# Gated delta rule on one core: VectorE's level 5 copies between the halves of q's convolution, TensorE's level 5 products ahead of the turned outputs

## Chip, cores and metric

The kernel runs on one core of a Trainium2 chip. The metric is the device time of one execution in microseconds (us); lower is better. The chip's engines are TensorE (PE in the rows; PEld is its weight load), VectorE (DVE), ScalarE (ACT), GpSimd (POOL) and SyncE (SP). Each takes its instructions in program order, and they wait for each other by semaphores.

## What is computed

The program is a stack of eight blocks on x (8 batches of 256 tokens, 128 features), each of the form x = x + layernorm(block(layernorm(x))). The change touches only the first, the gated delta rule attention. Cut to what matters:

```python
q, k = l2norm(silu(conv4(h @ w_q))), l2norm(silu(conv4(h @ w_k)))   # 16 heads of 64
v = silu(conv4(h @ w_v))                                            # 16 heads of 128
def step(S, inp):                       # one token
    q_t, k_t, v_t, g_t, b_t = inp
    S = S * exp(g_t)
    delta = (v_t - k_t @ S) * b_t
    S = S + outer(k_t, delta)
    return S, (q_t * scale) @ S
y = rmsnorm(o) * norm_w * silu(h @ w_g)
out = y @ w_out
```

conv4 is a causal convolution over four tokens, each feature with its own four taps.

## The kernel before

The function `gated_delta` (line 1869) works in chunks of 128 tokens (two in a batch, index `c`) with four heads at a time (`hg`). One unit of work is a quad: a batch and a group of four heads, 8 x 4 = 32 in all. `quads` (line 1922) writes the same pipeline into every engine: `step(x0, x1, x2, x3)` handles four quads at once, x0 being the newest and x3 the oldest. There are 35 steps; in 29 of them both x0 and x3 exist, and in the last three x0 is gone. Steps of the batches from the second on stand in a loop of four steps.

What sets the order of the work is the text of the five `step` functions, written out by hand: an engine does the calls in exactly that order. The parts that the change and the prediction touch are these.

- `project(x0, n)` on TensorE (line 1983): the projections of quad x0 into PSUM, n = 0 for q, 1 for k, 2 and 3 for v. Bank 4 holds n = 0 and 2, bank 5 holds n = 1 and 3. `project(x0, 2)` waits until ScalarE has copied both turned outputs out of bank 4 (semaphore `yT`).
- `tap3` on ScalarE (L2282) writes the fourth tap's share of the convolution into SBUF, two tiles of 128x256 (index `m`). `conv(x0, n)` on VectorE (L2544) adds the other three taps: for each tap two `scalar_tensor_tensor`, one for each m, and between taps a `drain`, because the next tap reads what the last one wrote. It then raises `conv`.
- The inverse of a 128x128 triangular matrix is put together from blocks of 16, of 32 and of 64; the code counts these as levels 4, 5 and 6. Of level 5: `merge_y(x2, 1, c)` on TensorE (L2083) multiplies into banks 0 and 1; `step_5(x2, c)` on VectorE (L2581, L2582) copies these to SBUF; `merge_t(x2, 1, c)` on TensorE (L2105) multiplies the copies into banks 2 and 3; `copy_t(x2, 1, c)` on ScalarE (L2334, L2335) brings them to SBUF; `turn_64` on VectorE (L2587) transposes a block. `merge_y(x2, 2, c)` (L2086) needs that for level 6.
- `turn_y(x0, x3, 1)` on TensorE (L2176): four transposes of x3's finished outputs into bank 4. It waits for `conv(x0, 0)`, which reads bank 4. `copy_y(x3, 1)` on ScalarE (L2381) takes them out. `out` on TensorE (L2189) multiplies them with `w_out` into bank 5; it waits for `copy_y(x3, 1)` and for `conv(x0, 1)`, which reads bank 5.
- `silu_qk` (L2295, with a table load of its own) and `square_qk` (L2302) on ScalarE follow the convolutions of q and k; between the two stands `tap3(x0, 2)`. `sum_squares` on TensorE (L2018) needs the squares.
- On SyncE and GpSimd the blocks of 16 are inverted; the order there is not touched.

ScalarE's order at this place is `tap3(x0, 1)`, `copy_y(x3, 1)`, `copy_t(x2, 1, 0)`, `copy_t(x2, 1, 1)`, `silu_qk(x0)`, `tap3(x0, 2)`, `square_qk(x0)`.

Of the kernel before, what the change touches and what calls it, by code (L numbers as in the profile page):

```python
# [1868 lines left out]
def gated_delta(k, add_y):  # L1869
# [13 lines left out]
    with Part(k) as p:  # L1883
# [29 lines left out]
        q = {n: p.sem(n) for n in names}  # L1913
# [3 lines left out]
        def wait(eng, name, n):  # L1917
            if isinstance(n, int) and n <= 0:
                return
            eng.wait_ge(q[name], n)  # L1920
# [14 lines left out]
        def first(x):  # L1935
            return isinstance(x[1], int) and x[1] == 0
# [7 lines left out]
        def halves_of(a, s):  # L1944

            a = a.rearrange("p (n two s) -> p n two s", two=2, s=s)
            return a[:, :, 0, :], a[:, :, 1, :]
# [4 lines left out]
        with nc.Block() as block:  # L1952
# [25 lines left out]
            def _(pe):  # L1978
# [110 lines left out]
                def merge_t(e, l, c):  # L2089
                    qe, b, hg = e  # L2090
                    s = (16, 32, 64)[l]
                    wait(pe, "Ystep", 6 * qe + 2 * l + c + 1)
                    if l == 2:
                        wait(pe, "TTc", 4 * qe + c + 1)
                    pe.sem_inc(q["through_pe"], 1)
                    for h in range(HG):
                        cols = slice(h * 64, (h + 1) * 64)
                        t = TT[:, hg % 2, c, h, :]
                        if l == 0:
                            i = mm(k.bank[2 + c][:, cols].rearrange("p (n s) -> p n s", s=s), step4[:, c, h, :], halves_of(t, s)[1],  # L2100
                                   start=True, stop=True)
                        elif l == 1:
                            for n in range(2):
                                r = slice(64 * n, 64 * n + 64)
                                i = mm(k.bank[2 + c][r, h * 64 + 32 * n:h * 64 + 32 * n + 32], step5[r, c, h, r],  # L2105
                                       t[r, 64 * n + 32:64 * n + 64], start=True, stop=True)
                        else:
                            i = mm(k.bank[2 + c][0:64, cols], step6[64:, c, h, 0:64], t[64:, 64:], start=True, stop=True)
                    i.then_inc(q["TTps"], 1)
# [54 lines left out]
                def turn_y(a, e, c):  # L2164
                    qe = e[0]
                    wait(pe, "y", 2 * qe + c + 1)
                    if c == 0:
                        wait(pe, "gate", 2 * qe + 1)
                        if a is not None:
                            wait(pe, "vtok", 2 * a[0] + 1)  # L2170
                    elif a is not None:
                        wait(pe, "conv", 4 * a[0] + 1)
                    else:
                        wait(pe, "yT", 2 * qe + 1)
                    for h in range(HG):
                        i = tr(hd(4, h), v[:, e[2], c, h, :], k.ident[:])  # L2176
                    i.then_inc(q["yTps"], 1)
# [23 lines left out]
                def step(x0, x1, x2, x3):  # L2201
                    if x0:
                        decays(x0, 0)
                    if x3:
                        turn_y(x1, x3, 0)
                    if x1:
                        turn_v(x1, 1)
                    if x2:
                        merge_y(x2, 0, 0)
                        merge_y(x2, 0, 1)  # L2210
                        merge_t(x2, 0, 0)
                        merge_t(x2, 0, 1)
                    if x0:
                        project(x0, 0)
                        decays(x0, 1)
                    if x3 and x3[2] == 0 and not first(x3):
                        turn_out(x1, x3[1] - 1)
                    if x2:
                        merge_y(x2, 1, 0)
                        merge_y(x2, 1, 1)  # L2220
                    if x0:
                        project(x0, 1)
                    if x3:
                        turn_y(x0, x3, 1)
                    if x2:
                        merge_t(x2, 1, 0)
                        merge_t(x2, 1, 1)
                    if x0:
                        project(x0, 2)
                    if x3:  # L2230
                        out(x0, x1, x3)
                    if x2:
                        merge_y(x2, 2, 0)
                        merge_y(x2, 2, 1)
                        merge_t(x2, 2, 0)
                    if x0:
                        sum_squares(x0)
                    if x2:
                        solve(x2, 0)
                        project_gate(x0, x2, 0)  # L2240
                    if x0:
                        turn_norms(x0)
                        turn_k(x0)
                        project(x0, 3)
                    if x2:
                        merge_t(x2, 2, 1)
                    if x0:
                        products(x0, 0)
                    if x2:
                        state(x2)  # L2250
                        outputs(x2, 0)
                        from_state(x2)
                    if x0:
                        products(x0, 1)
                    if x2:
                        solve(x2, 1)
                        project_gate(x0, x2, 1)
                    if x0:
                        turn_v(x0, 0)
                    if x2:  # L2260
                        outputs(x2, 1)
# [253 lines left out]
            def _(dve):  # L2515
# [17 lines left out]
                    dve.sem_inc(q["through_dve"], 1)  # L2533
                    vv.tensor_copy(xb[:], k.HT[:, bass.ds(b, 1), PAD:].rearrange("p a t -> p (a t)")).then_inc(q["xb"], 1)

                def conv(a, n):
                    qa, b, hg = a
                    wait(dve, "tap3", 4 * qa + n + 1)
                    first = (hg * 2, 8 + hg * 2, 16 + hg * 4, 18 + hg * 4)[n]
                    for j in (2, 1, 0):  # L2540
                        back = 3 - j
                        for m in range(2):
                            dst = (qk[:, hg, m], qk[:, hg, 2 + m], vT[:, m], vT[:, 2 + m])[n]
                            i = stt(out=dst[:, back:], in0=k.bank[4 + n % 2][:, m * T:(m + 1) * T - back],  # L2544
                                    scalar=taps[:, first + m, j:j + 1], in1=dst[:, back:], op0=ALU.mult, op1=ALU.add)
                        if j:
                            dve.drain()
                    i.then_inc(q["conv"], 1)

                def turn_blocks(e, name):  # L2550
                    hg = e[2]
# [38 lines left out]
                def step_6(e, c):  # L2590
                    wait(dve, "Yps", 6 * e[0] + 4 + c + 1)
                    vv.tensor_copy(step6[64:128, c, :, 0:64], packed(c, 64)[64:128, :, 0, :]).then_inc(q["Ystep"], 1)
# [77 lines left out]
                def step(x0, x1, x2, x3):  # L2670
                    if x0 and x0[2] == LAG:
                        load_x(x0)
                    if x2:
                        step_4(x2, 0)
                    if x3:
                        sum_o(x3, 1)
                    if x2:
                        step_4(x2, 1)
                        add_4(x2, 0)
                        add_4(x2, 1)  # L2680
                        dve.drain()
                        turn_blocks(x2, "T32")
                    if x3 and x3[2] == 0 and not first(x3):
                        copy_out(x3[1] - 1)
                    if x0:
                        conv(x0, 0)
                    if x2:
                        step_5(x2, 0)
                        step_5(x2, 1)
                    if x0:  # L2690
                        conv(x0, 1)
                    if x2:
                        turn_64(x2)
                        step_6(x2, 0)
                    if x0:
                        conv(x0, 2)
                    if x3:
                        add_y(x3)
                    if x2:
                        step_6(x2, 1)  # L2700
                    if x0:
                        norms(x0)
                        conv(x0, 3)
                        mask_products(x0, 0)
                    if x2:
                        subtract_memory(x2)
                        sum_o(x2, 0)
                    if x0:
                        mask_products(x0, 1)
                    if x1:  # L2710
                        turn_16(x1)
                    if x2:
                        add_o(x2)
# [768 lines left out]
```

## Time and profile before

| | us |
|---|---|
| three runs | 4843.22, 4853.23, 4852.27; median 4852.27 |
| the profiled execution: its own time | 4854.47 |
| its span in the profile | 4852.3 |
| steps with x0 and x3, start of `out` to the next start of `out` | 36.3 where nothing disturbs |
| VectorE busy in 400 to 600 us | 155.0 of 200 |
| TensorE busy in 400 to 600 us | 173.2 of 200 |

The gated delta rule lies between about 46 and 1310 us of the span. All rows come from one profiled execution. A row of the timeline gives start, duration, engine, line, operation, output and inputs, and the number of instructions that are merged in it; in brackets stands the idle time of the engine just before it and what ended that.

### The profile page before, as it was taken

To read this page: it belongs to the slowest core of one execution; us is meant where nothing else is said; L and a number is where in the kernel's file an instruction comes from. 1 tells how busy PE (TensorE), PEld (TensorE's weight loads), DVE (VectorE), ACT (ScalarE), POOL (GpSimd) and SP (SyncE) were. 2 spreads that over 40 slices of the span, in tenths; PEclk is the share of its full clock that TensorE was granted. 3 is DMA by queue.
4 is the path that set the end of the run, shared out by engine and by line. 5 is a ranking of instruction groups with operands and counts; after the bars stand their busy time and mean duration, and the time that the engine had idled before them with its cause. 6 is when DMAs were issued, how large, how long until landed. Compare 5 with 4: busy or idle time off the path is not lost. (4 is left out here: it accounts for less than half of the span.)

```text
span 4852.3 us, 76307 instructions
## 1 busy us (share of the span) xinstructions
PE 3918.1 (81%) x20245; PEld 2363.5 (49%) x20365; DVE 3743.4 (77%) x6391; ACT 2514.1 (52%) x5271; POOL 2862.3 (59%) x2779
## 2 busy tenths in 40 slices
PE   5888888888568678577989965888888868888885
PEld 3666666666456456466447742333333323333333
DVE  5777777777468478456058867999999889999996
ACT  3555555555344244323246644666666556666662
POOL 2555555555454044143023342999999559999992
PEclk7999999999778778788999986999999989999997
DMA  1000000000000000000000000000000000000000
GB/s 50 9 9 9 8 9 9 9 9 9 17 0 0 21 0 0 12 0 25 0 18 1 1 16 16 0 0 0 0 0 0 0 0 0 0 0 0 0 0 14
DMA packets 89949, 33.35 MB, mean 7 GB/s; under 512 B 78016, under 2 KB 85968, under 8 KB 88784
## 3 DMA queue, kind: packets, MB, share of 16 engines
q1 hardware_dynamic: 89680, 30.07, 2.6%
q8 instruction: 131, 2.15, 0.2%
q14 instruction: 138, 1.13, 0.1%
HBM read 24.79 MB, written 5.24 MB: 6 GB/s over the span
## 5 line engine op out<-in xcount | busy, mean ns | idle before, releaser
L3319 POOL TENSOR_TENSOR dBx<-dtx,b_row 128x1024 f32<-128x1024 f32 x512 | 1207.1, 2358 | 3.9 <-ACT b_row L3285 3.9
L3353 DVE TENSOR_TENSOR_SCAN h<-banks,dBx 128x1024 f32<-128x1024 f32 x512 | 1168.4, 2282 | 19.1 <-ACT banks L3279 19.1
L3237 PE MATMUL banks<-hc,ident 128*128 128x512 f32 x2048 | 965.5, 594 | 0.0
L3279 ACT ACTIVATE banks<-dt,alog 128x510 f32<-128x510 f32 x1024 | 661.6, 682 | 3.6 <-DVE h L3353 3.6
L3285 ACT ACTIVATE b_row<-banks 128x512 f32<-128x512 f32 x512 | 305.7, 597 | 575.8 <-PE banks L3221 575.8
L3237 PEld LDWEIGHTS banks<-hc,ident 128*128 128x128 f32 x2048 | 389.1, 190 | 271.9 <-issue 246.9
L3361 DVE TENSOR_TENSOR hc<-h,banks 128x768 f32<-128x768 f32 x512 | 478.4, 934 | 11.0 <-ACT c_row L3290 7.5
L3221 PE MATMUL banks<-bc_lo,selectors 128*128 128x512 bf16 x1024 | 391.9, 383 | 67.6 <-POOL b_row L3308 58.7
L3328 POOL TENSOR_TENSOR hc<-h,c_row 128x256 f32<-128x256 f32 x512 | 373.2, 729 | 63.2 <-ACT c_row L3290 29.3
L3220 PE MATMUL banks<-bc_hm_c,selectors 128*128 128x512 bf16 x506 | 195.2, 386 | 184.4 <-DVE hc L3361 184.3
L3220 PEld LDWEIGHTS banks<-bc_hm_c,selectors 128*128 (+1 forms) x512 | 49.2, 96 | 433.7 <-issue 433.6
L973 POOL TENSOR_TENSOR weighted<-probs,f 128x1024 f32<-128x1024 f32 x64 | 120.7, 1902 | 215.1 <-DVE f L1024 211.3
L2488 POOL TENSOR_TENSOR out_factors<-out_norms,exponents 128x4 f32<-128x4 f32 x64 | 64.4, 1007 | 289.1 <-DVE out_norms L2653 289.1
L3221 PEld LDWEIGHTS banks<-bc_lo,selectors 128*128 (+1 forms) x1024 | 99.7, 97 | 185.1 <-issue 168.4
L2544 DVE SCALAR_TENSOR_TENSOR qk<-banks,taps,qk 128x255 f32<-128x255 f32 (+2 forms) x384 | 167.2, 477 | 26.9 <-ACT qk L2282 15.4
L2544 DVE SCALAR_TENSOR_TENSOR v_featmajor<-banks,taps,v_featmajor 128x255 f32<-128x255 f32 (+2 forms) x384 | 167.3, 477 | 22.0 <-ACT v_featmajor L2282 11.4
L1642 POOL TENSOR_TENSOR squares<-qkv_ahead 128x1024 f32<-128x1024 f32 x32 | 60.9, 1904 | 183.9 <-ACT qkv_ahead L1578 183.9
L159 POOL MEMSET minus_half<- 128x4 f32 x7 | 0.7, 102 | 279.5 <-POOLq L365 162.9
L3220 PE MATMUL banks<-bc_hm_b,selectors 128*128 128x512 bf16 x398 | 153.0, 385 | 4.1 <-ACT b_row L3285 4.1
L2464 POOL TENSOR_TENSOR blocks_inv<-blocks_inv,block_products 64x14 f32<-64x14 f32 (+6 forms) x448 | 117.2, 262 | 63.7 <-issue 0.3
L2462 POOL TENSOR_TENSOR block_products<-blocks_inv,blocks 64x14 f32<-64x14 f32 (+6 forms) x448 | 114.0, 254 | 67.0 <-issue 5.5
L1211 POOL TENSOR_TENSOR norms<-norms,minus_half 128x64 f32<-128x64 f32 x8 | 84.7, 10593 | 105.9 <-DVE norms L1242 105.9
(448 smaller groups left out, 9091.8 us busy)
## 6 DMA issues: line engine op xcount, KB each, us to landing
delta_blocks<-A_turned SPq DMA_DIRECT2D x256, 8.0 KB, 1.5
inv_turned<-delta_blocks SPq DMA_DIRECT2D x256, 8.0 KB, 1.7
blocks<-delta_blocks SPq DMA_DIRECT2D x32, 64.0 KB, 2.1
delta_blocks<-blocks_inv SPq DMA_DIRECT2D x32, 64.0 KB, 1.9
wh<-in_l1f_wh SPq DMA_DIRECT2D x1, 2048.0 KB, 9.3
wqkv<-in_l0f_wqkv SPq DMA_DIRECT2D x2, 768.0 KB, 4.3
residual<-in_x SPq DMA_DIRECT2D x1, 1024.0 KB, 4.7
wv<-in_l0a_wv SPq DMA_DIRECT2D x1, 1024.0 KB, 7.5
```

The source lines that it names most:

```text
L973: nc.gpsimd.tensor_tensor(blocks(SW[:, u]), blocks(S[:, j % 2, u]), over(f[:, j % 2, 16 * u:16 * u + 16], T // NJ), ALU.mult).then_inc(wei ...
L2464: i = tt(U[:, 0:j, j + 1:], U[:, 0:j, j + 1:], tmp[:, 0:j, 0:n], ALU.add)
L2544: i = stt(out=dst[:, back:], in0=k.bank[4 + n % 2][:, m * T:(m + 1) * T - back], scalar=taps[:, first + m, j:j + 1], in1=dst[:, back:], op ...
L3220: nc.tensor.matmul(k.bank[bank], onto_all(sel[:, 0, bass.ds(n, 1)]), mem[part][:, cols], start=True, stop=False)
L3221: nc.tensor.matmul(k.bank[bank], onto_all(sel[:, which, bass.ds(n, 1)]), mem["lo"][:, cols], start=False, stop=True).then_inc(q[ready], 1)
L3237: i = nc.tensor.matmul(k.bank[e], k.ident[:], hc[:, s, e, :], start=False, stop=False)
L3279: i = nc.scalar.activation(a3[:, :, 1:], d3[:, :, 1:], ACT.Exp, scale=mem["A"][:, e, bass.ds(n, 1)])
L3285: nc.scalar.activation(bsb[:, s, :], k.bank[BBANK], ACT.Copy).then_inc(q["bsb_ready"], 1)
L3319: nc.gpsimd.tensor_tensor(dBx[:, s % NS], dtx[:, :, bass.ds(c * SCH, SCH)], across(bsb[:, s % NS, :], SE), ALU.mult).then_inc(q["dbx_ready ...
L3328: nc.gpsimd.tensor_tensor(hc[:, s % 2, :, DC:], h[:, s % NS, :, DC:], across(csb[:, s % 2, :], SE), ALU.mult).then_inc(q["hcp_ready"], 1)
L3353: v.tensor_tensor_scan(flat(h[:, s % NS]), flat(k.banks[:, at:at + SE, :]), flat(dBx[:, s]), 0.0, ALU.mult, ALU.add).then_inc(q["scanned"], 1)
L3361: v.tensor_tensor(hc[:, s % 2, :, 0:DC], h[:, s, :, 0:DC], across(k.bank[CBANK][:, 0:DC], SE), ALU.mult).then_inc(q["hc_ready"], 1)
```

## The change

On VectorE the two halves of `conv(x0, 0)` (m = 0 and m = 1) are done one after the other, and the four copies of `step_5` stand between them. A half is three `scalar_tensor_tensor` with a drain after the first and the second. The semaphore `conv` is raised after the second half. On TensorE `merge_t(x2, 1, 0)` and `merge_t(x2, 1, 1)` come before `turn_y(x0, x3, 1)` and not behind it. The other engines are as before.

```diff
@@ TensorE, step
                     if x0:
                         project(x0, 1)
-                    if x3:
-                        turn_y(x0, x3, 1)
                     if x2:
                         merge_t(x2, 1, 0)
                         merge_t(x2, 1, 1)
+                    if x3:
+                        turn_y(x0, x3, 1)
                     if x0:
                         project(x0, 2)
@@ VectorE
-                def conv(a, n):
+                def conv(a, n, parts=(0, 1)):
                     qa, b, hg = a
                     wait(dve, "tap3", 4 * qa + n + 1)
...
                     for j in (2, 1, 0):
                         back = 3 - j
-                        for m in range(2):
+                        for m in parts:
...
                         if j:
                             dve.drain()
-                    i.then_inc(q["conv"], 1)
+                    if 1 in parts:
+                        i.then_inc(q["conv"], 1)
@@ VectorE, step
                     if x0:
-                        conv(x0, 0)
+                        conv(x0, 0, (0,))
                     if x2:
                         step_5(x2, 0)
                         step_5(x2, 1)
                     if x0:
+                        conv(x0, 0, (1,))
                         conv(x0, 1)
```

## Rows read from the trace of the kernel before

**Rows 1.** The page's part 1: busy us, share of the span, instructions.

```profile
PE 3918.1 (81%) x20245; PEld 2363.5 (49%) x20365; DVE 3743.4 (77%) x6391; ACT 2514.1 (52%) x5271; POOL 2862.3 (59%) x2779
```

**Rows 2.** Waits from 100 to 1240 us: us in total, times, longest.

```profile
PE banks L2189 <- DVE qk L2544: 27.9, 29, 1.1
```

**Rows 3.** Timeline of TensorE, one step.

```profile
709.86 1.12 PE L2083 MATMUL banks<-inv,A_turned 64*64 64x32 f32 x32 [0.49 <-DVE inv L2554]
710.91 1.13 PE L2002 MATMUL banks<-norm_featmajor,wk 128*128 x4
712.57 0.66 PE L2176 MATMUL banks<-ident,v 128*128 128x128 f32 x4 [0.52 <-DVE qk L2544]
713.28 1.28 PE L2105 MATMUL banks<-inv_turned,steps 64*64 64x32 f32 x32
714.49 1.13 PE L2002 MATMUL banks<-norm_featmajor,wv 128*128 x4
716.61 1.99 PE L2189 MATMUL banks<-y_featmajor,wout 128*128 128x256 f32 x8 [0.99 <-DVE qk L2544]
718.53 1.14 PE L2086 MATMUL banks<-inv,A_turned 64*64 64x64 f32 x16
```

**Rows 4.** Timeline of VectorE, the same step.

```profile
707.41 0.42 DVE L2576 TENSOR_TENSOR inv_turned<-banks,inv_turned 128x256 f32<-128x256 f32 x1 [0.92 <-PE banks L2100]
707.93 1.79 DVE L2554 STREAM_TRANSPOSE inv<-inv_turned 32x256 f32<-32x256 f32 x4
709.75 2.76 DVE L2544 SCALAR_TENSOR_TENSOR qk<-banks,taps,qk 128x255 f32<-128x255 f32 x6
712.54 0.28 DVE L2581 COPY steps<-banks 32x128 f32<-32x128 f32 x1
...
713.46 0.30 DVE L2582 COPY steps<-banks 32x128 f32<-32x128 f32 x1
713.79 2.76 DVE L2544 SCALAR_TENSOR_TENSOR qk<-banks,taps,qk 128x255 f32<-128x255 f32 x6
716.58 0.43 DVE L2587 STREAM_TRANSPOSE inv<-inv_turned 32x256 f32<-32x256 f32 x1
```

**Rows 5.** Timeline of VectorE: the first three instructions of q's convolution, one by one.

```profile
709.75 0.48 DVE L2544 SCALAR_TENSOR_TENSOR qk<-banks,taps,qk 128x255 f32<-128x255 f32 x1
...
710.15 0.47 DVE L2544 SCALAR_TENSOR_TENSOR qk<-banks,taps,qk 128x255 f32<-128x255 f32 x1
...
710.70 0.48 DVE L2544 SCALAR_TENSOR_TENSOR qk<-banks,taps,qk 128x254 f32<-128x254 f32 x1
```

**Rows 6.** Timeline of ScalarE, the same step.

```profile
713.26 0.60 ACT L2381 ACTIVATE y_featmajor<-banks 128x512 f32<-128x512 f32 x1 [0.25 <-PE banks L2176]
713.97 0.27 ACT L2334 ACTIVATE inv_turned<-banks 32x128 f32<-32x128 f32 x1
...
715.16 1.28 ACT L2295 ACT_TABLE_LOAD   x1
716.59 1.06 ACT L2295 ACTIVATE qk<-qk 128x1024 f32<-128x1024 f32 x1
...
718.40 1.05 ACT L2302 ACTIVATE squares<-qk 128x1024 f32<-128x1024 f32 x1
```

**Rows 7.** Timeline of TensorE: the sum of squares in that step.

```profile
720.39 0.81 PE L2018 MATMUL banks<-squares,halves 128*8 128x256 f32 x3
```

**Rows 8.** Stretches around 599 us: length, engines busy, granted clock, DMA.

```profile
595.77:599.18 3.41, 2.28 (x38) 1.85 (x38) 3.14 (x10) 2.14 (x6) 2.16 (x9) 1.00 0.01 2
599.20:602.60 3.40, 3.10 (x8) 1.99 (x7) 2.12 (x5) 3.20 (x6) 2.30 (x8) 0.50 0.02 5
```

**Rows 9.** Timeline of TensorE at that place.

```profile
596.97 0.66 PE L2176 MATMUL banks<-ident,v 128*128 128x128 f32 x4 [1.07 <-DVE qk L2544]
...
598.89 1.82 PE L2002 MATMUL banks<-norm_featmajor,wv 128*128 x4
601.01 2.76 PE L2189 MATMUL banks<-y_featmajor,wout 128*128 128x256 f32 x8 [0.30 <-DVE qk L2544]
...
605.57 1.68 PE L2018 MATMUL banks<-squares,halves 128*8 128x256 f32 x7
```

**Rows 10.** Timeline of TensorE in the last steps, without x0.

```profile
1237.20 1.11 PE L2176 MATMUL banks<-ident,v 128*128 128x128 f32 x4
1238.24 1.92 PE L2105 MATMUL banks<-inv_turned,steps 64*64 64x32 f32 x32
1240.09 3.78 PE L2189 MATMUL banks<-y_featmajor,wout 128*128 128x256 f32 x8
```

## The prediction

> **What bounds the kernel now.** The page's busy shares come first [rows 1]: TensorE 81%, VectorE 77%. Neither is full, so the two must be handing a chain to each other, and the question is who waits for whom at the edited place. The waits answer it: `out` (L2189) waited for a convolution on VectorE 29 times, 27.9 us in all, nearly a microsecond each [rows 2]. The 29 are all the steps that have both x0 and x3.
>
> The timelines of one step show the place. On VectorE one stretch without a gap runs from 707.41, where TensorE released it, to 717.01: the last addition of level 4, its transposes, q's convolution at 709.75, the four copies of level 5 from 712.54 to 713.76, k's convolution from 713.79 to 716.55, and the transpose of 32 [rows 4]. On TensorE there are two idle gaps beside it: 0.52 us before `turn_y`, which waits for q's convolution, and 0.99 us before `out`, which waits for k's [rows 3]. After `out` TensorE goes on almost without a gap. So between 707.4 and 716.6 VectorE sets the time, and from 716.6 TensorE does. The gap ahead of `turn_y` lies inside the stretch where TensorE has a further 0.99 us to spare; it costs nothing today.
>
> **What is moved.** The copies start earlier by half a convolution, and the products (1.28 us [rows 3]) can run in the old gap. But `out` still waits for k's convolution, and that ends when VectorE has done the same instructions as before. I take the parts in turn.
>
> *The split of q's convolution, on the path.* Six instructions come in three pairs. Within a pair the second starts 0.40 us after the first (709.75, 710.15), though each takes 0.48; over a drain the next starts 0.55 us after (710.15 to 710.70) [rows 5]. Before, the way from the first start to the first copy is 0.40, 0.55, 0.40, 0.55, 0.40 and, from the last start to the copy, 0.50: 2.80 in all (the rows give 2.79, 709.75 to 712.54 [rows 4]). After, each half has two gaps of 0.55, since each instruction now has the drain behind it. First half: 0.55 + 0.55 + 0.50 = 1.60, copies at 711.35. The copies hold the engine 1.25 us (712.54 to 713.79 [rows 4]): second half at 712.60. Its third instruction starts at 713.70, and k's convolution, which does not depend on it, 0.40 later: 714.10 and not 713.79. So VectorE ends k's convolution 0.30 us later. That is 32 quads x 0.30 = 9.6 us, all on the path. From below, the drains could be hidden, 0; from above, a single instruction could pay its full 0.48 plus the 0.15 that the drain adds to 0.40, hence 0.63 a gap: 4 x 0.08 x 32 = 10 us more. I take 0.30, since 0.55 is measured on the same instruction with the same drain.
>
> [...]
>
> *Waits queued on VectorE.* The second half of q's convolution now stands behind `step_5`'s wait for `merge_y`. That ends at 710.98 [rows 3], and the copies are reached at 711.35, so nothing. Its own repeated wait is long satisfied.
>
> *TensorE up to `out`, covered.* The first product can start at about 712.0 (copies of c = 0 done at 711.9), the second after 712.6; they end near 713.25. Then `turn_y` waits: q's convolution now ends at 713.70 + 0.47 = 714.17, where it was 712.51, so `turn_y` starts at 714.22. `copy_y` started 0.69 us after `turn_y` (712.57, 713.26 [rows 3, 6]): 714.91 to 715.51. `project(x0, 2)` must wait for it, as both use bank 4: 715.57 to 716.70. `out` wants k's convolution, 716.85, and starts at 716.91. So the later transposes are hidden by 0.2 us; if that cover were gone, each further 0.1 us would cost 2.9 us in all.
>
> *ScalarE, nearly on the path.* `copy_t` stands behind `copy_y`: it moves to 715.5, the four copies take 1.1 us, and then the table load (1.28), which was over just in time at 716.44, ends at 717.8. `silu_qk` starts there, 0.95 us later than k's convolution would let it. From the start of `silu_qk` to the end of the squares is 2.86 us (716.59 to 719.45 [rows 6]), so squares are ready at 720.66. `sum_squares` would be reached by TensorE at 720.39 + 0.30 = 720.69 [rows 7]. A tie: 0, at most 0.1 x 29 = 3 us. `turn_64` needs `copy_t` by 716.9 and gets it at 716.5: nothing.
>
> *The last steps.* Without x0 the products (1.92) and the transposes (1.11 [rows 10]) change places, and `out` must wait for a copy of 0.6 us behind the transposes: about 0.7 us in each of two steps, 1.4.
>
> *The clock.* Before `out` TensorE's granted clock sometimes falls to 1.2 GHz. In the stretch ending at 599.18 TensorE was busy 2.28 us of 3.41, with a gap of 1.07 before `turn_y`, and in the next the granted clock is 0.50 [rows 8, 9]. It happened in 2 of the 29 steps. The price: `out` to `sum_squares` took 4.56 us (601.01 to 605.57) against 3.78 (716.61 to 720.39) [rows 7, 9], so 0.78 each, and `project(x0, 2)` took 1.82 and not 1.13 us [rows 3, 9]. After the change the gaps in this place are 0.97 and 0.68 and 0.2 us, with only the small products and four transposes between the two projections, which stand 3.5 us apart (2.45 before: 712.04 to 714.49). That is thinner work than in any of the steps before, so I expect the fall in about half of the 29 steps, at 0.8 us or a little more as the slow projection now eats its 0.2 us cover: 14 x 0.9 = 13 us. Falls elsewhere in the step (at the start of level 4) shift with the step's length; I take 2 us back for these. Net 11, between -5 and +25.
>
> The sum: 9.6 + 1.4 + 0 + 11 = 22 us. The profiled execution took 4854.5, which is 2.2 above the median shown; on the median of 4852.3 this gives **4874 us**.
>
> **The rivals.**
> 1. *The split alone costs, and the clock stays as it is.* 4852.3 + 11 = 4863. For it: the longest single gap is 0.97 us and these exist today. Against: there are now two of them. 18%.
> 2. *Clock and ScalarE together.* The clock falls in nearly every step and the squares are late: 29 x 1.0 + 3 + 11 = 43, 4895. 8%.
> 3. *Faster: the filled gap counts.* If the 0.52 us ahead of `turn_y` were on the path, 29 x 0.52 = 15 us would come back, less the split: 4848, or 4837 with a free split. It decides from the point where k's convolution is ready before TensorE reaches `out`, so that TensorE and not VectorE sets its start. Rows 2 and 3 show the opposite in all 29 steps. A shift of the clock's falls could do the same. 6%. The Trainium skill says ("Perfetto Trace Analysis", Optimizing Scalar/DVE Operations) that breaking up instructions can help where VectorE is not saturated but leaves bubbles on others; over the whole span it isn't, in these 9.6 us it is.
> 4. *It does nothing: drains are free and everything else is covered.* 4852 to 4856. [...] 10%.
> The forecast has the remaining 58%, with its own range 4866 to 4883.
>
> **The numbers.** A measurement of this kernel can tell about 0.2% (9.7 us) from no change, so "same" is 4842.6 to 4862.0. Faster: rival 3, 6%. Same: rival 4 and something under half of rival 1, 17%. Slower: the rest, 77%. The range from 4857 to 4888 leaves out rivals 2 and 3 and part of 4.
>
> **What would show it.** In the changed profile: single instructions of q's convolution 0.55 us apart; k's convolution starting 4.35 us after q's (4.04 before [rows 4]); the wait of `turn_y` (L2176) for L2544 near 1 us and not 0.5; a new wait of L2002 for `copy_y`; `silu_qk` right behind its table load; steps of 36.6 us where nothing disturbs, 36.3 before; and more stretches at clock 0.50 just before `out`. If `out` no longer waits for L2544, or undisturbed steps keep their length, the forecast's reasons are wrong.

## The result and the profile after

The changed kernel takes 4915.78 us (median of four runs, 4909.88 to 4921.96), the kernel before 4852.75 (four runs, 4843.22 to 4856.25). The ratio is 1.0133 with a 95% interval of 1.0113 to 1.0153: 63 us slower, where 22 us were forecast. The direction was right; the time lies outside the range. Of all executions behind this document one, of the kernel e2 below, was in a slower state (8530.74 us); it counts in no median and no ratio.

The page after (busy us; the span in 40 slices, PEclk is the granted TensorE clock in tenths), to set against [rows 1]:

```profile
PE 3971.1 (81%) x20245; PEld 2401.0 (49%) x20365; DVE 3747.6 (76%) x6391; ACT 2511.4 (51%) x5271; POOL 2862.8 (58%) x2779
PEclk7999988999868788779899987899999989999997
```

VectorE has the same 6391 instructions and 4 us more work. TensorE has the same number of instructions too, yet is busy 53 us longer. Work that stays equal and takes longer points to the clock. Here is the same stretch, 124 to 1200 us, in both kernels (the third last number is the granted clock as a share of 2.4 GHz). Before:

```profile
124.00:1200.00 1076.00, 937.03 (x7416) 689.06 (x7416) 820.45 (x2283) 609.25 (x1379) 616.21 (x1222) 0.97 0.06 9
```

After:

```profile
124.00:1200.00 1076.00, 933.84 (x6967) 687.80 (x6965) 772.15 (x2139) 571.22 (x1295) 579.96 (x1160) 0.91 0.05 8
```

In the same time TensorE did 449 fewer matmuls (6%) while it was equally busy; VectorE did 144 fewer instructions.

**A step in which the clock stays up** is as forecast, but for one gap on VectorE. TensorE after, around 510 us, to set against [rows 3]:

```profile
506.42 1.13 PE L2002 MATMUL banks<-norm_featmajor,wk 128*128 x4
507.60 1.28 PE L2105 MATMUL banks<-inv_turned,steps 64*64 64x32 f32 x32
510.12 0.66 PE L2176 MATMUL banks<-ident,v 128*128 128x128 f32 x4 [1.24 <-DVE qk L2544]
511.56 1.10 PE L2002 MATMUL banks<-norm_featmajor,wv 128*128 x4 [0.78 <-ACT y_featmajor L2381]
512.80 1.99 PE L2189 MATMUL banks<-y_featmajor,wout 128*128 128x256 f32 x8
...
516.68 1.89 PE L2018 MATMUL banks<-squares,halves 128*8 128x256 f32 x8
```

The products now run at once, and the gap has moved: 1.24 us before `turn_y` and a new 0.78 us before `project(x0, 2)`, which waits for the copy. VectorE in that step, to set against [rows 4]:

```profile
505.25 1.59 DVE L2544 SCALAR_TENSOR_TENSOR qk<-banks,taps,qk 128x255 f32<-128x255 f32 x3
506.86 0.28 DVE L2582 COPY steps<-banks 32x128 f32<-32x128 f32 x1
...
508.11 1.04 DVE L2544 SCALAR_TENSOR_TENSOR qk<-banks,taps,qk 128x255 f32<-128x255 f32 x2
509.59 3.16 DVE L2544 SCALAR_TENSOR_TENSOR qk<-banks,taps,qk 128x253 f32<-128x253 f32 x7 [0.44 <-issue]
512.78 0.43 DVE L2588 STREAM_TRANSPOSE inv<-inv_turned 32x256 f32<-32x256 f32 x1
```

The second and third instruction of the first half, looked at one by one as in [rows 5]; the first starts at 505.25:

```profile
505.81 0.48 DVE L2544 SCALAR_TENSOR_TENSOR qk<-banks,taps,qk 128x254 f32<-128x254 f32 x1
...
506.37 0.48 DVE L2544 SCALAR_TENSOR_TENSOR qk<-banks,taps,qk 128x253 f32<-128x253 f32 x1
```

These starts are 0.56 us apart. The step has one thing more: the row at 509.59 shows VectorE idle for 0.44 us in the middle of the second half, and what ended that is "issue", so it waited for nothing that the profile shows. It is no accident of this step. Between the last addition of level 4 and `out`, on the stretch where VectorE sets the time, the kernel before has no such gap in any of its 29 steps. The changed one has 18, in 18 steps, of 0.43 to 0.49 us: 14 inside q's convolution and 4 ahead of a copy that comes just before it. A start over a drain then comes 0.92 us after the last one and not 0.56, so such a gap costs 0.36 us. Here is one ahead of the copy, from e3 below, and then the same copy before:

```profile
916.51 0.42 DVE L2679 COPY block_out<-banks 128x256 f32 x1 [0.48 <-issue]
746.08 0.42 DVE L2668 COPY block_out<-banks 128x256 f32 x1
```

ScalarE in that step, to set against [rows 6]:

```profile
510.82 0.60 ACT L2381 ACTIVATE y_featmajor<-banks 128x512 f32<-128x512 f32 x1 [2.31 <-PE banks L2176]
...
512.43 1.28 ACT L2295 ACT_TABLE_LOAD   x1
513.72 1.06 ACT L2295 ACTIVATE qk<-qk 128x1024 f32<-128x1024 f32 x1
...
515.53 1.05 ACT L2302 ACTIVATE squares<-qk 128x1024 f32<-128x1024 f32 x1
```

`silu_qk` starts right behind its table load and 0.92 us after `out`; the squares end at 516.58, and `sum_squares` starts at 516.68, 3.88 us after `out`. Before, this was 3.76 to 3.88. So ScalarE costs next to nothing.

**A step in which the clock falls** looks like this. TensorE, one step later, to set against [rows 7, 9]:

```profile
546.78 0.66 PE L2176 MATMUL banks<-ident,v 128*128 128x128 f32 x4 [0.88 <-DVE qk L2544]
548.21 2.04 PE L2002 MATMUL banks<-norm_featmajor,wv 128*128 x4 [0.78 <-ACT y_featmajor L2381]
550.05 3.62 PE L2189 MATMUL banks<-y_featmajor,wout 128*128 128x256 f32 x8
...
555.89 1.89 PE L2018 MATMUL banks<-squares,halves 128*8 128x256 f32 x8
```

Its stretches, as in [rows 8]:

```profile
544.12:547.50 3.38, 2.39 (x39) 1.61 (x37) 3.14 (x9) 1.02 (x4) 2.12 (x9) 1.00 0.01 2
547.53:550.90 3.37, 2.69 (x6) 2.18 (x7) 2.18 (x5) 3.29 (x7) 2.23 (x9) 0.50 0.02 5
550.95:554.30 3.35, 3.35 (x14) 2.34 (x12) 0.00 (x0) 2.27 (x4) 2.07 (x9) 0.50 0.01 2
554.36:557.70 3.34, 3.10 (x28) 1.75 (x26) 2.88 (x7) 0.38 (x1) 2.05 (x3) 1.00 0.11 22
```

The granted clock is 0.50, that is 1.2 GHz, from 547.5 to 554.3. The projection takes 2.04 us and not 1.10, and only behind it `out` can start, 1.84 us after the projection's start and not 1.24: 0.60 us late, though k's convolution had been done for 0.65 us. Then `out` takes 3.62 and not 1.99, and `sum_squares` comes 5.84 us after `out` and not 3.88. This one step loses 0.60 + 1.96 = 2.56 us.

The waits from 100 to 1290 us show the handover (us in total, times, longest), to set against [rows 2]:

```profile
PE banks L2176 <- DVE qk L2544: 27.3, 29, 1.3
PE banks L2002 <- ACT y_featmajor L2381: 22.5, 29, 0.8
...
PE banks L2189 <- DVE qk L2544: 0.2, 1, 0.2
```

`out` waited 27.9 us for the convolution before, and 0.2 after: now the projection ends just before it, or, in 19 of the 29 steps, k's convolution has been done for 0.59 us or more when `out` starts.

**Where the time went.** The starts in the timelines cut each step into three parts. Summed over the 28 steps from the first `out` to the 29th, in us (e2 and e3 are told below):

| part | before | e2 | after | e3 |
|---|---|---|---|---|
| `out` to `sum_squares` | 108.1 | 116.7 | 134.5 | 107.9 |
| `sum_squares` to `project(x0, 1)` | 781.3 | 760.5 | 793.7 | 777.0 |
| `project(x0, 1)` to `out` | 161.0 | 177.4 | 190.9 | 180.4 |
| steps of 29 with the clock at 0.50 near `out` | 2 | 15 | 24 | 2 |

"Near `out`" is from 3 us before it to `sum_squares`. The middle part holds nothing that the change touches, and still it is 12.4 us longer after the change.

### The profile page after: what moved, and what is told of

The parts are those of the page before. It is cut to its first block and busy times, and to the rows that moved or that the text cites. A ratio compares the mean times of both kernels' runs of the same rounds, so it can differ in the third digit from the quotient of the medians.

```text
span 4920.0 us, 76371 instructions
## 1 busy us (share of the span) xinstructions
PE 3971.1 (81%) x20245; PEld 2401.0 (49%) x20365; DVE 3747.6 (76%) x6391; ACT 2511.4 (51%) x5271; POOL 2862.8 (58%) x2779
```

## The experiments

The theory after the result: the time went to TensorE's clock, which falls because the work between the projections of k and of v has become thin. The rivals: the drains of the split cost the time; the later copies on ScalarE do; the new order holds up the chain even at full clock. Unread matmuls ("fillers") serve as a probe: `fill(bank, widths)` multiplies a constant weight tile into PSUM columns that nobody reads, in a bank that is free at that time. Ratios are to the kernel before on the same chip, with 95% intervals; times in the tables are medians. The times of 28 steps, the clocks and the counts of steps come from one profiled execution of each kernel, and while the executions of one kernel differ by up to some 30 us, how much its 28 steps differ was not measured.

### First series: what of the change carries the loss

TensorE's new order alone (against the changed kernel):

```diff
-                        conv(x0, 0, (0,))
+                        conv(x0, 0)
...
-                        conv(x0, 0, (1,))
```

> Only TensorE's order is changed (products of level 5 ahead of turn_y); VectorE does q's convolution whole, then the copies. Clock theory: the products wait for copies that end at 713.8 of the step of before, so turn_y, its copy and project(x0, 2) come late too, the two projections stand about 3.8 us apart with thin work between, and out starts about 0.4 us later; 12 us by that wait and 40 to 60 us by a granted clock of 0.50 around out in more than half of the 29 steps: 4900 to 4925 in all. Theory of the split (the drains cost it): without the split the time is near that of before, 4852 to 4865. Theory of ScalarE's chain (copy_t late, squares late): 0.6 us in each step, 17 us, 4870.

The split alone (against the changed kernel):

```diff
                         conv(x0, 0, (0,))
+                        conv(x0, 0, (1,))
                     if x2:
                         step_5(x2, 0)
                         step_5(x2, 1)
                     if x0:
-                        conv(x0, 0, (1,))
                         conv(x0, 1)
...
+                    if x3:
+                        turn_y(x0, x3, 1)
                     if x2:
                         merge_t(x2, 1, 0)
                         merge_t(x2, 1, 1)
-                    if x3:
-                        turn_y(x0, x3, 1)
```

> Only the split: the two halves of q's convolution one behind the other, then the copies, TensorE's order as before. It prices the drains alone. Clock theory: 0.30 us in each of 32 quads, 9.6 us, 4862, with a clock like that of before (about 12 falls in this part). Theory of the split: most of the 63 us, above 4890. If drains are free: 4852.

The changed kernel with its gaps filled:

```diff
+                def fill(bank, *widths):
+                    at = 512 - sum(widths)
+                    for n in widths:
+                        mm(k.bank[bank][:, at:at + n], wq[:, 0:P], wq[:, 0:n], start=True, stop=True)
+                        at += n
...
                         merge_t(x2, 1, 1)
+                    if x0 and x3:
+                        fill(0, 128, 128)
                     if x3:
                         turn_y(x0, x3, 1)
+                    if x0 and x3:
+                        fill(0, 256)
```

> The changed kernel with matmuls that nobody reads in TensorE's two gaps before out: two of 128 columns ahead of turn_y, one of 256 behind it (0.43 us each, inside waits of 0.97 and 0.68 us). Nothing else moves. Clock theory: the falls before out go away, out starts as late as k's convolution lets it, and 9.6 us of the split and a few us of the tail are left: 4860 to 4872. Theory of ScalarE's chain or of the split: filling idle TensorE time changes nothing, 4910 to 4920, or more if the fillers are in the way.

The kernel before with a filler elsewhere:

```diff
+                    if x0 and x2:
+                        fill(7, 256, 128)
                     if x2:
                         merge_y(x2, 0, 0)
```

> The kernel of before with matmuls that nobody reads (256 and 128 columns, 0.64 us) in TensorE's gap of 0.86 us ahead of the first product of level 4, where most of its falls of the clock begin. Clock theory: some 8 of its 12 falls go away, at 1.5 to 3 us each: 4825 to 4842. If the clock is worth little here: 4850 to 4856, or above where a filler holds up the product behind it.

Measured:

| kernel | us | ratio (95%) | clock, 124 to 1200 us | 28 steps, us | low near `out`, of 29 |
|---|---|---|---|---|---|
| before | 4852.75 | | 0.97 | 1050.4 | 2 |
| after | 4915.78 | 1.0133 (1.0113 to 1.0153) | 0.91 | 1119.0 | 24 |
| e1, TensorE's order alone | 4917.94 | 1.0131 (1.0114 to 1.0148) | 0.92 | 1109.1 | 20 |
| e2, the split alone | 4858.92 | 1.0016 (1.0003 to 1.0028) | 0.97 | 1054.5 | 15 |
| e3, after, filled | 4866.41 | 1.0033 (1.0020 to 1.0046) | 0.97 | 1065.3 | 2 |
| e4, before, filled ahead of level 4 | 4852.67 | 0.9992 (0.9982 to 1.0002) | 0.99 | 1045.6 | 0 |

The last column but one is the time from the first start of `out` to the 29th in the profiled execution. It holds 28 steps of the pipeline and leaves the rest of the program out. The last column counts the steps with the clock at 0.50 near `out`, as above.

e3 decides. The fillers stand inside waits and bring TensorE more work, and the kernel gets about 50 us faster (ratio 1.0033 and not 1.0133). TensorE in a step of e3 in which the clock stays up (L2204 is the filler):

```profile
501.06 1.28 PE L2105 MATMUL banks<-inv_turned,steps 64*64 64x32 f32 x32
502.27 0.71 PE L2204 MATMUL banks<-wq 128*128 128x128 f32 x4
503.58 0.66 PE L2176 MATMUL banks<-ident,v 128*128 128x128 f32 x4 [0.60 <-DVE qk L2554]
504.08 0.60 PE L2204 MATMUL banks<-wq 128*128 128x256 f32 x2
505.02 1.10 PE L2002 MATMUL banks<-norm_featmajor,wv 128*128 x4 [0.34 <-ACT y_featmajor L2391]
506.25 1.99 PE L2189 MATMUL banks<-y_featmajor,wout 128*128 128x256 f32 x8
```

From the projection of v to `out` it is 1.23 us, as in the undisturbed step of the changed kernel (1.24), so the fillers moved nothing there. The whole stretch of e3:

```profile
124.00:1200.00 1076.00, 952.95 (x7464) 697.54 (x7464) 809.80 (x2245) 597.60 (x1358) 607.23 (x1207) 0.97 0.06 9
```

The table of parts says where the 53.7 us of 28 steps that e3 gives back had been. About 37 lie between `project(x0, 1)` and `sum_squares`, where the fillers stand. The other 17 lie in the middle part: in three steps after the change the clock is at 0.50 for 13.7 us on end behind the loop's branch, in e3 at most for 10.2. Why fillers ahead of `out` help there too is not shown.

e2 was to give the split its price: the runs say 0.16%, 8 us (1 to 14), where 9.6 were forecast. But its trace shows that this is a sum of things that cancel. From `project(x0, 1)` to `out` its 28 steps take 16.4 us more than before: 9.0 for the drains (0.32 in each of 28 steps, for the shortest undisturbed ones take 36.65 us here and 36.33 before), and the rest mostly for 14 issue gaps like those above. From `out` to `sum_squares` they take 8.6 more, since the clock is low there in 15 steps and not in 2. And the middle part takes 20.8 less, since the clock is at 0.50 for 10 us in it and not for 58. TensorE in a step of e2 that has an issue gap ahead of the copy on VectorE:

```profile
605.58 0.66 PE L2176 MATMUL banks<-ident,v 128*128 128x128 f32 x4 [1.76 <-DVE qk L2544]
...
609.70 2.32 PE L2189 MATMUL banks<-y_featmajor,wout 128*128 128x256 f32 x8
```

The longest wait of `turn_y` for VectorE was 1.4 us before. So the split by itself already brings the clock down near `out`; what is ruled out is that its drains cost most of the 63 us. e1 shows that the loss does not need the split at all. It holds a wait as well as the clock. One of its steps at full clock:

```profile
587.22 1.13 PE L2002 MATMUL banks<-norm_featmajor,wk 128*128 x4
589.58 1.28 PE L2105 MATMUL banks<-inv_turned,steps 64*64 64x32 f32 x32 [1.24 <-DVE steps L2583]
...
593.17 1.89 PE L2189 MATMUL banks<-y_featmajor,wout 128*128 128x256 f32 x8
...
597.32 1.90 PE L2018 MATMUL banks<-squares,halves 128*8 128x256 f32 x8 [0.40 <-ACT squares L2302]
```

From `project(x0, 1)` to `out` it takes 5.95 us, 5.70 before [rows 3], and from there to `sum_squares` 4.15 and not 3.88. That is 0.52 x 28 = 15 us of the 58.7 that its 28 steps take more, which leaves some 44 for the clock.

e4 is a miss: 4853 and not 4825 to 4842. Its clock is at 0.99, the best yet, and the time is that of before. TensorE in e4 around one of the loop's branches:

```profile
475.08 1.72 PE L2010 MATMUL banks<-g_masked,tri 128*128 128x512 f32 x2 [2.55 <-issue]
...
478.72 0.88 PE L2204 MATMUL banks<-wq 128*128 128x256 f32 x4
479.43 1.90 PE L2078 MATMUL banks<-inv,A_turned 128*128 128x64 f32 x16
```

Once in four steps TensorE stands still for 2.5 to 3.1 us for its own instructions ("issue"), the clock is at 0.50 behind that in e4 too, and the filler, which starts without a wait there, is on the path.

### Second series: is it the work in the gap?

Four more kernels. TensorE's order alone, with the fillers of e3 (the diffs of e1 and e3 together):

> TensorE's new order with VectorE's old one, plus the same unread matmuls ahead of and behind turn_y. Clock theory: the falls before out go away and what is left is the wait: out comes 0.3 to 0.4 us later in each of 29 steps, 4862 to 4870. A rival in which the order itself holds up the chain (late copy_t, squares, level 6): still above 4900.

A smaller dose:

```diff
                         merge_t(x2, 1, 1)
+                    if x0 and x3:
+                        fill(0, 128)
                     if x3:
                         turn_y(x0, x3, 1)
```

> The changed kernel with one unread matmul of 128 columns (0.21 us) ahead of turn_y and no other. Clock theory: a smaller dose leaves part of the falls: between the changed kernel and the filled one, 4875 to 4910. A theory in which fillers act in another way than by the work in the gap would give either of the two ends.

The same dose where TensorE is busy (in the changed kernel):

```diff
                     if x3:
                         out(x0, x1, x3)
+                    if x0 and x3:
+                        fill(0, 128, 128, 256)
```

> Control: the changed kernel with the same unread matmuls (0.86 us), but right behind out, where TensorE is busy. Clock theory: the falls before out stay, and the fillers are on the path: 4916 + 29 x 0.86 = 4941, within 10. If more TensorE work in a step is enough, wherever it stands: 4895 or less.

VectorE's part of the change alone (against the changed kernel, on TensorE `turn_y` again ahead of the products):

```diff
+                    if x3:
+                        turn_y(x0, x3, 1)
                     if x2:
                         merge_t(x2, 1, 0)
                         merge_t(x2, 1, 1)
-                    if x3:
-                        turn_y(x0, x3, 1)
```

> VectorE's part of the change alone: copies between the halves, TensorE's order as before. turn_y waits for the second half (1.66 us later than before) and the products now stand behind it, so project(x0, 2) comes about 1.6 us later and out some 0.2 us after k's convolution lets it. Clock theory: projections 4 us apart, falls as often as in the changed kernel: 4905 to 4930. Without an effect of the clock: 9.6 + 29 x 0.2 = 15 us, 4868.

Measured:

| kernel | us | ratio (95%) | clock, 124 to 1200 us | 28 steps, us | low near `out`, of 29 |
|---|---|---|---|---|---|
| e5, TensorE's order, filled | 4904.65 | 1.0117 (1.0086 to 1.0149) | 0.95 | 1092.9 | 18 |
| e6, after, one filler | 4907.91 | 1.0120 (1.0090 to 1.0151) | 0.92 | 1101.7 | 18 |
| e7, after, filler behind `out` | 4908.28 | 1.0117 (1.0085 to 1.0148) | 0.95 | 1105.8 | 12 |
| e9, VectorE's part alone | 4944.04 | 1.0201 (1.0169 to 1.0233) | 0.90 | 1135.9 | 27 |

e6 lies between the two ends in its 28 steps, near the upper one (1101.7, between 1119.0 and 1065.3), and has fewer steps with a low clock near `out` (18, between 24 and 2). The runs can't tell it from the changed kernel: 1.0120 against 1.0133, with intervals that overlap.

e5 misses: 4905, not 4862 to 4870. TensorE in one of its steps:

```profile
502.48 1.13 PE L2002 MATMUL banks<-norm_featmajor,wk 128*128 x4
504.84 1.28 PE L2105 MATMUL banks<-inv_turned,steps 64*64 64x32 f32 x32 [1.24 <-DVE steps L2593]
506.05 0.71 PE L2204 MATMUL banks<-wq 128*128 128x128 f32 x4
506.60 0.60 PE L2176 MATMUL banks<-ident,v 128*128 128x128 f32 x4
...
507.98 1.10 PE L2002 MATMUL banks<-norm_featmajor,wv 128*128 x4 [0.34 <-ACT y_featmajor L2391]
508.92 1.89 PE L2189 MATMUL banks<-y_featmajor,wout 128*128 128x256 f32 x8
...
513.07 1.25 PE L2018 MATMUL banks<-squares,halves 128*8 128x256 f32 x5 [0.30 <-ACT squares L2312]
```

Without the split the products wait 1.24 us for the copies, a gap ahead of the fillers that they don't fill, and the clock is only at 0.95. At full clock two things cost time. The first is e1's wait, 0.52 us. The second is the filler itself: in e1 `out` starts 3.59 us after the products (589.58 to 593.17), here 4.08 (504.84 to 508.92), for q's convolution has long been done and `turn_y` follows the first filler without a wait. So 0.49 us of the filler are on the path. Together this is 1.01 of the 1.03 us by which e5's shortest full steps (37.36 us) are longer than those of before (36.33), and 1.03 x 28 = 29 us of the 42.5 that its 28 steps take more. e5 is thus no clean test: some 14 us of its time are the probe's own.

e7 misses as a control: neither 4941 nor 4895 or less came out. 25 us of fillers came onto the path (`sum_squares` 4.76 us after `out`, not 3.88, in steps without a fall), but the falls became fewer: 12 steps near `out` and not 24. Its steps take 37.53 us where nothing disturbs. Why the falls were fewer here is open; the steps also have another length. In e3 the length of a full-clock step can't be the reason: it is 36.65 us there, and e10 below has the same (36.67) and keeps the falls.

e9 is worst, and a miss too: 4944, above the 4905 to 4930 expected, with the clock low near `out` in 27 of 29 steps. `turn_y`, the products and the projection all queue behind the second half; in its step around 602 us TensorE stands idle for 1.71 us ahead of `turn_y`.

### Third series: a better control, and a better kernel

The fillers of e3 with 8 columns each, so `fill(0, 8, 8)` and `fill(0, 8)`:

> Control for the filled kernel: the same number of unread matmuls at the same places, but 8 columns wide and not 128 or 256, so hardly any work. Clock theory: the falls before out stay, 4905 to 4925. If it is the extra instructions that help (weights loaded earlier, another order of waits): 4860 to 4872, as in the filled kernel.

The fillers of e4 in three steps of four, on the kernel before (`if x0 and x2 and x0[2]:` in place of `if x0 and x2:`):

> The kernel of before with the unread matmuls (0.64 us) ahead of level 4 in three steps of four: not in the step after the loop's branch, where TensorE stood still for 2.5 to 3.1 us anyway, the clock fell in spite of the filler and the filler itself ran on the path at half the clock. Clock theory: the six falls of 6.8 us at 1.53 us each stay away and nothing is given back: 4840 to 4848. If those falls are covered by other waits: 4850 to 4856.

The changed kernel with the fillers of e3 and of e8:

> The changed kernel with both sorts of fillers: around turn_y, and ahead of level 4 in three steps of four. Clock theory: the costs add up: the split's 9.6 us and the tail's 1 to 2 us on the kernel of before, less the 6 to 10 us that the fillers ahead of level 4 gave there: 4852 to 4860. If something else of the change costs on top of split and clock: above 4865.

Measured:

| kernel | us | ratio (95%) | clock, 124 to 1200 us | 28 steps, us | low near `out`, of 29 |
|---|---|---|---|---|---|
| e10, after, tiny fillers | 4911.87 | 1.0111 (1.0071 to 1.0152) | 0.92 | 1109.5 | 21 |
| e8, before, filled in three of four | 4845.47 | 0.9989 (0.9978 to 1.0000) | 0.99 | 1040.4 | 1 |
| e11, after, both fillers | 4865.48 | 1.0013 (0.9997 to 1.0030) | 0.97 | 1068.8 | 2 |

e10 has the same number of extra instructions at the same places as e3, and the loss stays. Its stretch:

```profile
124.00:1200.00 1076.00, 951.71 (x7177) 707.21 (x7176) 778.55 (x2154) 574.42 (x1303) 581.51 (x1161) 0.92 0.05 8
```

It is the work of the fillers that counts, not their presence; whether it must stand in the gap, e7 leaves open. e8 has the lowest ratio of all: its 28 steps are 10.0 us shorter than before, and the runs say 0.11% faster, with an interval that just reaches 1. It is no measurable gain over the kernel before, and clearly better than the changed kernel. e11 does not decide what it was meant to. Its median of 4865.48 is just above the mark of 4865. By the ratio of 1.0013, which is 6 us, it would be 4859 on the kernel before at 4852.75, within what was expected, for the kernel before had a median of 4859.12 on this chip. The interval, 0.9997 to 1.0030, holds both. Its 28 steps show no gain over e3. They take 28 us more than e8's: 9.0 are the drains, about 7.5 by estimate the 21 issue gaps of its trace at 0.36 us, and in three of them the clock is at 0.50 for 13.7 us on end behind the branch, which none of the 28 steps of e8 or of the kernel before shows.

## Why the prediction was wrong

*What bounds.* Right for the kernel before: VectorE set the start of `out` in all 29 steps, so the early products brought nothing. In the changed kernel that holds where the clock stays up; in 19 steps it is TensorE's own projection, at half clock, that `out` follows.

*The split.* The drains are right: 0.30 us in a quad was forecast, from gaps of 0.55. The gaps are 0.56, and e3's and e11's shortest full steps are 36.65 us against 36.33. The term as a whole is too small. The issue gaps are missing in it, 18 x 0.36 = 6.5 us by estimate, so that the split costs about 15.5 us in the 28 steps and not 9. That e2's runs show 8 us beside a forecast of 9.6 is luck, as its parts show. The Trainium skill ("VectorE: DVE Perf Modes", The DRAIN you can't avoid) says that the next operation does not start until the pipe is empty, and also that one which is not held, that is, not made to wait for all earlier ones, starts earlier. The starts 0.40 us apart under a duration of 0.48 agree with the second; what an explicit drain adds, 0.15 to 0.16 us, is measured here.

*ScalarE.* Right: a tie was forecast, and in steps at full clock `sum_squares` starts at most 3.88 us after `out`, as before, without a wait for the squares.

*TensorE up to `out`.* Right in steps at full clock: the new wait for the copy is 22.5 us in all, and it is hidden. The forecast saw that a projection at half clock would eat the cover of 0.2 us, but put only 0.1 us on that. It takes the cover and 0.60 us more.

*The last steps.* A wait of about 0.7 us before `out` in each of two steps was expected. It is there in both, 0.69 us; here is the first:

```profile
1312.15 3.64 PE L2189 MATMUL banks<-y_featmajor,wout 128*128 128x256 f32 x8 [0.69 <-ACT y_featmajor L2381]
```

*The clock.* This is the step that failed, the term "14 x 0.9 = 13 us" and with it "Net 11, between -5 and +25". The mechanism is the right one, and its size is off by a factor of five. The 28 steps take 68.6 us more. Of these 9.0 are the drains and about 6.5 the issue gaps. The other 53 are the clock, by estimate, and e3, which keeps drains and gaps, gives back 53.7. Three things were mis-sized.

- How often: "in about half of the 29 steps"; it was 24 of the 29.
- How much: 0.8 to 0.9 us was the price of the one fall that I had looked at, in which the clock was back 1.6 us after the start of `out` [rows 8, 9]. In the changed kernel it is often low twice as long, 6.8 us, and one step lost 2.56 us. Against the kernel before, the part behind `out` is 26.4 us longer and the part ahead of it 29.9, of which 15.5 are drains and issue gaps. That leaves 41 us over 24 steps, about 1.7 us each.
- Elsewhere: "I take 2 us back for these". The middle part of the steps lost 12.4 us instead. The steps with the loop's branch carry all of it.

Stretches of 6.8 us at 0.50 stood in the trace of before, in another place of the step, and should have set the upper bound. Rival 2, the clock in nearly every step, came nearest, with too low a price of 1.0 us, nothing for the rest of the step, and a ScalarE term that was not needed. A slip besides: the range from 4857 is said to leave out "part of 4", but rival 4, 4852 to 4856, lies wholly below it.

What stays open is why the clock falls where it does. That thin work between the two projections brings it down fits e3, e6 and e10. But e2, with TensorE's old order, has 15 low steps near `out`, and in e7 work elsewhere halved them. So the lost time is shown to go with the clock; that the thin place alone causes the falls is argued.

## What to carry over

Where TensorE sets the time of a stretch, ask of each reordering what it does to TensorE's work just ahead of that stretch, not only to its waits. Here small matmuls were moved out of a gap, and in 24 of 29 steps TensorE ran at 1.2 GHz near `out`. A quick probe is to put unread matmuls into the waits: if the kernel gets faster, and with very narrow ones it does not, it was the clock. See in the trace that they are inside the waits; in e5 one was not. When you price a fall of the clock, let the range reach to the longest one in the trace, and count the falls of the whole step. And a control that comes out near its forecast can do so by two errors: compare it part by part, as e2.

## What was not expected of the hardware

- The granted clock fell to 0.50 behind gaps of 0.88 and 0.78 us with 0.66 us of transposes between them; no idle gap of TensorE at `turn_y` or the projection was over 1.3 us in the changed kernel.
- Unread work that takes about 0.9 us when nothing covers it (e7), put inside the waits of each step (e3), took 50 us off the kernel. The same instructions 8 columns wide took off nothing that can be told (e10, 1.0111 against 1.0133, intervals overlapping).
- Every trace with q's convolution in two halves has issue gaps of 0.43 to 0.49 us on the stretch where VectorE sets the time (in 29 steps e2 has 14, after and e9 18, e3 and e10 19, e6, e7 and e11 21); those with it whole (before, e1, e4, e5, e8) have none. What makes them is not shown.
- A higher clock need not be a shorter time: e4 went from 0.97 to 0.99 and stayed at the same time. Behind the loop's branch, where TensorE stands still for about 2.5 to 3.1 us once in four steps, the filler itself was paid at half clock.
- Two independent operations on VectorE start 0.40 us apart though each takes 0.48; with a drain between them it is 0.55 to 0.56.
